# A decoder block with 9984 large float32r products: their operands laid at other distances modulo 512 bytes

## The chip, the cores and the metric

One core of one Trainium2 chip runs the whole program. The metric is the device time of one execution in microseconds, the median of three runs.

## What is computed

The input x is 32 sequences of 64 tokens, 512 wide (2048 tokens). Three layers are added to it in turn, each on a layer norm of what stands before it:

```python
x = x + attn(layernorm(x))    # a state space layer (Mamba-2 form), 128 heads of 64, 8 groups
x = x + xattn(layernorm(x))   # attention over 64 context tokens, 32 heads, 8 key/value heads
x = x + ffn(layernorm(x))     # four low-rank experts of rank 16, the two best by a router
```

The first layer is nearly all of the work:

```python
proj = input_states @ in_proj_w.T                  # 512 -> 8192 gate, 10240 xBC, 128 dt
xBC = silu(conv(xBC, 4 taps) + conv_b)             # 8192 x, 8 x 128 B, 8 x 128 C
dt = softplus(dt + dt_bias)
y = ssd(x, -exp(A_log), B, C, D, dt)               # causal over the 64 tokens, in chunks of 32
g = y * silu(gate)
g = g * rsqrt(mean of g*g in each of 8 groups + eps) * norm_w
return g @ out_w.T                                 # 8192 -> 512
```

## The kernel before, in words

The 2048 tokens are cut into four blocks of 512 (`tb`), and each block goes through the eight groups of the state space layer (`g`): 32 iterations `n`, in the order of the two Python loops of `iterations`. An iteration has 18 units of 128 projected channels: B, C, and eight pairs of x and gate. Each engine has one queue written out by hand, with semaphores between them, in the function `body` of its block; nothing is scheduled by a planner.

On TensorE an iteration holds, interleaved with each other:

- `unit(k, ...)`, line 538: a unit is a sum of 12 products of the helper `mm` (L472), 128x128 stationary by 128x512 moving, into one PSUM bank. Weights and normalised tokens are each split into a high and a low float32r part, and three of the four pairs are multiplied (`for w, a in ((0, 0), (0, 1), (1, 0))`) over four slices of the 512 inner channels. The stationary operand is a slice of `w_ring`, the moving one a slice of `xnb0` in even blocks and of `xnb1` in odd ones. 32 x 18 x 12 = 6912 products. In the first iteration four units go to the banks `p_out`, 48 products; the others go to `p_in`.
- `project(c, ...)`, line 789 (and 881 at the end): the output product. The stationary operand is a 128-token slice of the gated rows, `g_hi` (twice) and `g_lo` (once); the moving one is 512 columns of the output weights in `o_ring`. 12 products for each of eight `c`, 32 x 8 x 12 = 3072.
- `heads`, `state_products`, `to_tokens` (transposes of `x_t` against `id_sb`, L562), `mean_squares` (`ss` against `ones`) and, in `slot`, the pieces of the second and third layer (tiles `..._l`).
- `step_sizes(b)`, line 490, once a block: 12 products of the same form, `wd` stationary and `xnb` moving.

In block 0 the weights come raw from memory: SyncE loads `raw_w` (five slots, so five units ahead), ACT casts the high part into `w_ring` (six slots), POOL makes the low part (L1848), and SyncE stores both for the later blocks, which load `w_ring` directly. `o_ring` is filled in the same manner from `raw_o`.

A tensor is laid in each partition's memory in the order of its `sb(...)` call; `ExitStack`s give back ranges, so that the tiles of the second and third layer at the end (`tail`) overlay the loop's. `sb` aligns to 64 bytes (32 for tensors under 256 bytes) unless `align` is given:

```python
w_ring = sb("w_ring", [P, RING_W, 2, KT, P], F32R, align=2048)
xnb = [sb(f"xnb{b}", [P, 2, KT, TB], F32R, align=2048) for b in range(2)]
o_ring = sb("o_ring", [P, RING_O, 2, HID], F32R, align=2048)
g_hi = sb("g_hi", [P, 2, TB], F32R, align=2048)
g_lo = sb("g_lo", [P, 2, TB], F32R, align=2048)
```

Every slice of these tensors that a product reads is a multiple of 512 bytes from the tensor's start (128 or 512 elements of 4 bytes), so its place modulo 512 is the tensor's. "Distance" in this text is the moving operand's start less the stationary one's, modulo 512:

| product | stationary, mod 512 | moving, mod 512 | distance |
|---|---|---|---|
| units, all blocks | w_ring 0 | xnb 0 | 0 |
| output | g_hi, g_lo 0 | o_ring 0 | 0 |
| step sizes | wd 320 | xnb 0 | 192 |

Of the kernel before, what the change touches and what calls it, by code (L numbers as in the profile page):

```python
# [7 lines left out]
P = 128  # L8
NSEQ, SEQ, HID = 32, 64, 512
TOKENS = NSEQ * SEQ  # L10
KT = HID // P
# [3 lines left out]
CPG = INTER // GROUPS // P  # L15
TB = 512
NTB = TOKENS // TB
SPB = TB // SEQ
QT = TB // P
# [4 lines left out]
KV, REP, HD = 8, 4, 16  # L24
EXPERTS, RANK = 4, 16
LORA_SCALE = 16.0 / 16.0 ** 0.5
MIDW = EXPERTS * RANK
# [6 lines left out]
RING_W, RING_O = 6, 4  # L34
# [4 lines left out]
def decoder_kernel(nc, x, ctxv, amask, wt, wdt, owt, params, dtb, alog, ffa, ffb,  # L39
                   ident, c_mask, c_bd, c_v2, c_eq, out):  # L40
    F32, F32R = mybir.dt.float32, mybir.dt.float32r
# [8 lines left out]
    with outer:  # L50
        def alloc(stack):
            def sb(name, shape, dt=F32, align=None):
                wide = 4 * int(np.prod(shape[1:])) >= 256
                return stack.enter_context(nc.sbuf_tensor(name, shape, dt, align_bytes=align or (64 if wide else 32)))
            return sb

        def sem(name):
            return outer.enter_context(nc.semaphore(name))

        sb = alloc(outer)  # L60
# [7 lines left out]
        wa = sb("wa", [P, KT, MIDW + EXPERTS])  # L68
        cmask = sb("cmask", [P, SEQ])
        cpar = sb("cpar", [P, 5 * CONVS])  # L70
        dpar = sb("dpar", [P, CPG])
        dts = sb("dts", [P, QT, HPG])
        msv = sb("msv", [P, QT])
        rms = sb("rms", [P, QT])
        st6 = sb("st6", [P, QT, 6])
        mv = sb("mv", [P, QT, 2])
        ve = sb("ve", [P, QT])
        rstd = sb("rstd", [P, QT])
        spare = sb("spare", [P, 1])
        dtbs = sb("dtbs", [P, 1])  # L80
        als = sb("als", [P, 1])
        nega = sb("nega", [P, 3])
        acb = sb("acb", [P, 2, QT, HID], align=2048)
        wb = sb("wb", [MIDW, HID])

# [7 lines left out]
        sb = alloc(main)  # L93
# [2 lines left out]

        loop = ExitStack()
        sb = alloc(loop)
        xnb = [sb(f"xnb{b}", [P, 2, KT, TB], F32R, align=2048) for b in range(2)]
        dtk = sb("dtk", [P, 2, QT, HEADS])  # L100
        cumk = sb("cumk", [P, 2, QT, HEADS])
        decay = sb("decay", [P, 2, 8, QT, SEQ])
# [5 lines left out]
        sg = sb("sg", [P, GATES, TB])  # L108
        t_y = sb("t_y", [P, 2, TB])
        g_f = sb("g_f", [P, 2, TB])  # L110
        o_ring = sb("o_ring", [P, RING_O, 2, HID], F32R, align=2048)
        g_hi = sb("g_hi", [P, 2, TB], F32R, align=2048)
        g_lo = sb("g_lo", [P, 2, TB], F32R, align=2048)
        g_sq = sb("g_sq", [P, 2, TB])
        ss = sb("ss", [P, TB])
        cbt = sb("cbt", [P, QT, SEQ])
# [5 lines left out]
        d_s = sb("d_s", [P, TB])  # L122
        cum = sb("cum", [P, TB])

        VW = 2 * HD + 2
        TILE_WIDE = (("sc", [2, 2, 2 * KV // 2, SEQ]), ("row", [HID]), ("col", [KT, P]), ("x2s", [HID]))
        TILE_REST = (("p_t", [REP, KV // 2, P]), ("ctx", [P]), ("ctx_t", [P]), ("v2r", [2, P]), ("v2", [2, KV // 2, VW]), ("kbd", [2, KV // 2, SEQ]),
                     ("mid", [MIDW + EXPERTS]), ("midg", [MIDW]), ("m_t", [P]), ("mx", [REP * KV]), ("sm", [REP * KV]), ("rs", [REP * KV]),
                     ("st", [6]), ("mv", [2]), ("ve", [1]), ("rd", [1]), ("nm", [1]), ("nb", [1]), ("pw", [EXPERTS * EXPERTS]), ("pe", [EXPERTS * EXPERTS]),
                     ("rank", [EXPERTS]), ("lmax", [1]), ("gates", [EXPERTS]), ("gsum", [1]))  # L130
        Tile = namedtuple("Tile", [name for name, _ in TILE_WIDE + TILE_REST])

        def tile_part(sb, part, tag):
            return {name: sb(f"{name}_{tag}", [MIDW if name == "m_t" else P] + shape) for name, shape in part}

        rest = tile_part(sb, TILE_REST, "l")
        raw = ExitStack()
        sb = alloc(raw)
        raw_w = sb("raw_w", [P, RAW_W, KT * P])
        raw_o = sb("raw_o", [P, RAW_O, HID + 1])  # L140
        raw.close()
        wide = ExitStack()
        loop_tile = Tile(**tile_part(alloc(wide), TILE_WIDE, "l"), **rest)
        wide.close()
        loop.close()
# [2 lines left out]

        tail = ExitStack()
        sb = alloc(tail)  # L150
        tail_tiles = [Tile(**tile_part(sb, TILE_WIDE, q), **tile_part(sb, TILE_REST, q)) for q in range(QT)]
        tail.close()

        const_in = sem("const_in"); const_cp = sem("const_cp"); par_in = sem("par_in")
# [315 lines left out]
        def _(pe):  # L470
            def mm(o, l, r, first, last):
                return nc.tensor.matmul(o, lhsT=l, rhs=r, start=first, stop=last)  # L472
# [242 lines left out]
            def values_totals(q, t, S, banks):  # L715
# [4 lines left out]
                for r in range(REP):  # L720
                    for gp in range(KV // 2):
                        at = (r % 2 * (KV // 2) + gp) * VW
                        for s in range(2):
                            rows = slice(s * SEQ, (s + 1) * SEQ)
                            ins = mm(banks[r // 2][rows, at:at + VW], S.p_t[:, r, gp, rows], S.v2[:, s, gp, :], True, True)
                ins.then_inc(pv_done, 1)
# [213 lines left out]
        def _(act):  # L940
            def copy(dst, src, func=ACT.Copy, **kw):
                return nc.scalar.activation(dst, src, func, **kw)  # L942
# [296 lines left out]
            def ones_out(S):  # L1239
                by_pair = v2m[:, 0:2 * HD:HD].unsqueeze(1)  # L1240
                for s in range(2):
                    ins = copy(S.v2[:, s, :, 2 * HD:VW], by_pair.broadcast_to([P, KV // 2, 2]))
                ins.then_inc(v1_done, 1)
# [53 lines left out]
        def _(dve):  # L1297
# [4 lines left out]
            def link(ins):  # L1302

                own[0] += 1
                ins.then_inc(dve_own, 1)
                dve.wait_ge(dve_own, own[0])
# [313 lines left out]
            def attended_totals(t, S, banks):  # L1620

                dve.wait_ge(pv_done, t + 1)
                by_pair = [bank[:, 0:2 * (KV // 2) * VW].rearrange("p (r g c) -> p r g c", r=2, g=KV // 2) for bank in banks]
                for b in range(2):
                    ins = V.reciprocal(S.rs[:, b * 2 * KV:(b + 1) * 2 * KV].rearrange("p (r g e) -> p r g e", r=2, g=KV // 2),
                                       by_pair[b][:, :, :, 2 * HD:VW])
                link(ins)
# [445 lines left out]
```

## Time and profile before

| | |
|---|---|
| median of three runs | 2847.14 us (2843.8 to 2848.58) |
| the profiled execution's own time | 2843.42 us |
| its span, first to last instruction | 2841.6 us |
| granted TensorE clock over the span | 0.997 |
| TensorE matmuls | 22298, busy 2804.8 us |
| TensorE weight loads | 22298, busy 2274.4 us |
| VectorE (DVE) / ScalarE (ACT) / GpSimd (POOL) busy | 1990.1 / 1462.6 / 1315.5 us |
| mean transfer rate | 203 GB/s |

The profile is of one execution, taken by the hardware. A matmul's own time overlaps with that of the next one, so the sum of a group's busy time counts each stretch once, and the mean time of one matmul is longer than the step from its start to the next start. Weight loads stand as an engine of their own (PEld), since they run beside the matmul before them. In the chain of waits each piece of time is put to what ended last there.

### The profile page before, as it was taken

How to read it: one execution, taken by the hardware profiler on the slowest of the kernel's cores; microseconds unless marked ns; L12 is line 12 of the kernel's file. 1: busy time of each engine (PE TensorE's matmuls, PEld its weight loads, DVE VectorE, ACT ScalarE, POOL GpSimd, SP SyncE). 2: the span in 40 equal slices, each digit the busy share in tenths (PEclk: the TensorE clock that was granted, in tenths of full speed). 3: DMA queues.
4: the chain of work that ended last, by engine and by line, in shares of the span. 5: the costliest groups of instructions: out<-in, count | busy, mean ns of one | idle time of the engine just before them, and what ended most of it. 6: DMA issues, size and time to landing. Idle time of an engine off the chain costs nothing.

```text
span 2841.6 us, 56494 instructions
## 1 busy us (share of the span) xinstructions
PE 2804.8 (99%) x22298; PEld 2274.4 (80%) x22298; DVE 1990.1 (70%) x3152; ACT 1462.6 (51%) x2205; POOL 1315.5 (46%) x840
## 2 busy tenths in 40 slices
PE   7999999999999999999999999999999999999998
PEld 5788888878788788887888888888888888878886
DVE  8777768887667757677676766677666666666767
ACT  5666656655445545445445454544545444453545
POOL 4766767775344333443343443424434334343334
PEclk9999999999999999999999999999999999999999
DMA  7788777778565555565665665555656656555530
GB/s 253 274 298 300 264 270 258 269 257 291 181 200 189 181 183 182 181 192 182 203 193 180 200 189 174 186 180 185 203 180 192 193 173 203 181 184 187 186 130 31
DMA packets 179428, 578.27 MB, mean 203 GB/s; under 512 B 25248, under 2 KB 31904, under 8 KB 171104
## 3 DMA queue, kind: packets, MB, share of 16 engines
q1 hardware_dynamic: 179168, 574.66, 61.5%
q8 instruction: 180, 2.95, 0.4%
q14 instruction: 80, 0.66, 0.1%
HBM read 460.29 MB, written 114.29 MB: 202 GB/s over the span
## 4 chain that ended last, share of the span: by engine, by line
PE 91%; DVE 6%; ACT 1%; issue 1%; DMA 0%; POOL 0%; SPq 0%; DVEq 0%; ACTq 0%; POOLq 0%
PE p_in L472 53%; PE p_out L472 23%; PE p_y L472 9%; PE p_in L562 4%; DVE cv L1430 1%; PE p_y L700 1%; DVE o_ring L1370 1%; DVE t_y L1479 0%; DVE g_f L1491 0%; DVE mx L1600 0%; ACT cv L942 0%; DVE sc L1587 0%; DVE cum L1392 0%; DMA raw_w<-wt 0%; DVE decay L1462 0%
## 5 line engine op out<-in xcount | busy, mean ns | idle before, releaser
L472 PE MATMUL p_in<-xnb,w_ring 128*128 128x512 f32 x6864 | 1673.2, 396 | 1.8 <-DVE cv L1430 0.9
L472 PEld LDWEIGHTS p_in<-xnb,w_ring 128*128 128x128 f32 x6864 | 1260.8, 188 | 262.6 <-issue 2.7
L1430 DVE SCALAR_TENSOR_TENSOR cv<-p_in,cpar,cv 128x504 f32<-128x504 f32 x954 | 699.8, 734 | 469.2 <-ACT cv L942 445.4
L1856 POOL TENSOR_TENSOR g_lo<-g_f,g_hi 128x512 fp32r<-128x512 f32 x256 | 338.1, 1322 | 1195.8 <-ACT g_hi L942 1195.8
L472 PE MATMUL p_out<-o_ring,g_hi 128*128 128x512 f32 x2048 | 638.3, 393 | 1.7 <-POOL g_lo L1856 1.7
L942 ACT ACTIVATE cv<-p_in,cpar 128x512 f32<-128x512 f32 x318 | 246.6, 775 | 636.9 <-PE p_in L472 600.5
L472 PEld LDWEIGHTS p_out<-o_ring,g_hi 128*128 128x128 f32 x2048 | 379.4, 188 | 80.3 <-issue 2.3
L472 PE MATMUL p_out<-o_ring,g_lo 128*128 128x512 f32 x1024 | 399.6, 390 | 0.0
L1467 DVE TENSOR_TENSOR x_tok<-p_in,dts 128x512 f32<-128x512 f32 x256 | 176.5, 689 | 285.7 <-PE p_in L562 284.0
L942 ACT ACTIVATE x_t<-cv 128x512 f32<-128x512 f32 x256 | 160.9, 628 | 309.9 <-DVE t_y L1479 285.9
L1867 POOL TENSOR_TENSOR ss<-ss,g_sq 128x512 f32<-128x512 f32 x190 | 310.3, 1633 | 7.4
L1911 POOL TENSOR_TENSOR decay<-decay,cumk 128x2048 f32<-128x2048 f32 x63 | 234.8, 3727 | 38.9 <-DMA decay<-cum_scr 37.7
L942 ACT ACT_TABLE_LOAD x183 | 234.8, 1283 | 4.0 <-PEq L2067 0.7
L1848 POOL TENSOR_TENSOR w_ring<-raw_w,w_ring 128x512 fp32r<-128x512 f32 x144 | 209.2, 1477 | 51.5 <-ACT w_ring L942 35.8
L942 ACT ACTIVATE sg<-p_in 128x512 f32<-128x512 f32 x254 | 149.3, 588 | 160.9 <-PE p_in L472 160.9
L472 PEld LDWEIGHTS p_out<-o_ring,g_lo 128*128 128x128 f32 x1024 | 192.2, 188 | 40.7
L1479 DVE SCALAR_TENSOR_TENSOR t_y<-x_t,dpar,p_y 128x256 f32<-128x256 f32 x512 | 210.9, 474 | 1.1 <-PE p_y L472 1.1
L1491 DVE TENSOR_TENSOR g_f<-t_y,sg 128x512 f32<-128x512 f32 x256 | 180.2, 744 | 0.1
L942 ACT ACTIVATE g_hi<-g_f 128x512 fp32r<-128x512 f32 x256 | 159.2, 623 | 32.8 <-DVE g_f L1491 32.3
L472 PEld LDWEIGHTS p_y<-decay,x_tok 64*64 64x64 f32 x8192 | 131.1, 134 | 46.2 <-issue 46.2
L562 PE MATMUL p_in<-id_sb,x_t 128*128 128x128 f32 x1024 | 158.7, 278 | 7.1 <-ACT x_t L942 5.2
L562 PEld LDWEIGHTS p_in<-id_sb,x_t 128*128 128x128 f32 x1024 | 118.2, 141 | 51.5 <-issue 20.6
(258 smaller groups left out, 2251.4 us busy)
## 6 DMA issues: line engine op xcount, KB each, us to landing
w_ring<-ws_scr SPq DMA_DIRECT2D x432, 512.0 KB, 3.7
o_ring<-ows_scr SPq DMA_DIRECT2D x192, 512.0 KB, 4.6
ws_scr<-w_ring SPq DMA_DIRECT2D x144, 512.0 KB, 5.9
decay<-cum_scr SPq DMA_DIRECT2D x126, 512.0 KB, 6.7
raw_w<-wt SPq DMA_DIRECT2D x144, 256.0 KB, 5.1
ows_scr<-o_ring SPq DMA_DIRECT2D x64, 512.0 KB, 6.3
raw_o<-owt SPq DMA_DIRECT2D x64, 256.5 KB, 5.6
acb<-x SPq DMA_DIRECT2D x3, 1024.0 KB, 7.7
```

The costliest lines, as they stand in the source:

```text
L472: return nc.tensor.matmul(o, lhsT=l, rhs=r, start=first, stop=last)
L562: ins = nc.tensor.transpose(p_in[1][:, q * P:(q + 1) * P], x_t[:, c % 2, q * P:(q + 1) * P], id_sb[:, :])
L700: ins = nc.tensor.transpose(banks[rl][:, gp * P:(gp + 1) * P], pv, id_sb[:, :])
L942: return nc.scalar.activation(dst, src, func, **kw)
L1430: ins = V.scalar_tensor_tensor(acc[:, :, t:SEQ], src[:, :, 0:SEQ - t], cpar[:, 5 * m + 3 - t:5 * m + 4 - t], acc[:, :, t:SEQ], ALU.mult, A ...
L1467: V.tensor_tensor(x_tok[:, c % 2, :, :].rearrange("p q (h d) -> p q h d", h=2), p_in[1][:, :].rearrange("p (q h d) -> p q h d", q=QT, h=2) ...
L1479: ins = V.scalar_tensor_tensor(t_y[:, c % 2, :].rearrange(by_seq, q=QT, s=2)[:, s], x_t[:, c % 2, :].rearrange(by_seq, q=QT, s=2)[:, s], d ...
L1491: V.tensor_tensor(g_f[:, c % 2, :], t_y[:, c % 2, :], sg[:, (CPG * n + c) % GATES, :], ALU.mult).then_inc(g_done, 1)
L1848: T(w_ring[:, k % RING_W, 1, :, :].rearrange("p k c -> p (k c)"), raw_w[:, (UNITS * g + k) % RAW_W, :], w_ring[:, k % RING_W, 0, :, :].rea ...
L1856: T(g_lo[:, c % 2, :], g_f[:, c % 2, :], g_hi[:, c % 2, :].bitcast(F32), ALU.subtract).then_inc(glo_done, 1)
L1867: T(ss[:, :], a, g_sq[:, c % 2, :], ALU.add).then_inc(ss_done, 1)
L1911: T(decay[:, blk, :, :, :], decay[:, blk, :, :, :], last.unsqueeze(3).broadcast_to([P, 8, QT, SEQ]), ALU.subtract) \
```

## The change

The tensors are laid out anew; nothing else is touched. The small tensors `ve`, `rstd`, `spare`, `dtbs` (128 bytes together) come before `xnb0`, `st6` and `mv` (128 bytes) between `xnb0` and `xnb1`, and `dpar`, `msv`, `rms`, `als` (128 bytes) between `o_ring` and `g_hi`. The alignment to 2048 falls away for `xnb`, `o_ring`, `g_hi` and `g_lo`, and stays for `w_ring` and `acb`. Five small tiles of the second and third layer (`mx`, `sm`, `rs`, `pw`, `pe`) move ahead of `acb`, into the room that the others left.

```diff
-        xnb = [sb(f"xnb{b}", [P, 2, KT, TB], F32R, align=2048) for b in range(2)]
+        xnb = []
         ve = sb("ve", [P, QT])
         rstd = sb("rstd", [P, QT])
         spare = sb("spare", [P, 1])
         dtbs = sb("dtbs", [P, 1])
+        xnb.append(sb("xnb0", [P, 2, KT, TB], F32R))
+        st6 = sb("st6", [P, QT, 6])
+        mv = sb("mv", [P, QT, 2])
+        xnb.append(sb("xnb1", [P, 2, KT, TB], F32R))
...
-        o_ring = sb("o_ring", [P, RING_O, 2, HID], F32R, align=2048)
-        g_hi = sb("g_hi", [P, 2, TB], F32R, align=2048)
-        g_lo = sb("g_lo", [P, 2, TB], F32R, align=2048)
+        o_ring = sb("o_ring", [P, RING_O, 2, HID], F32R)
+        dpar = sb("dpar", [P, CPG])
+        msv = sb("msv", [P, QT])
+        rms = sb("rms", [P, QT])
+        als = sb("als", [P, 1])
+        g_hi = sb("g_hi", [P, 2, TB], F32R)
+        g_lo = sb("g_lo", [P, 2, TB], F32R)
...
+        loop_small = tile_part(sb, TILE_SMALL, "l")
         acb = sb("acb", [P, 2, QT, HID], align=2048)
         wb = sb("wb", [MIDW, HID])
...
-        rest = tile_part(sb, TILE_REST, "l")
+        rest = {**tile_part(sb, TILE_REST, "l"), **loop_small}
```

The places that come out of it:

| product | stationary, mod 512 | moving, mod 512 | distance |
|---|---|---|---|
| units, even blocks (0, 2) | w_ring 0 | xnb0 128 | 128 |
| units, odd blocks (1, 3) | w_ring 0 | xnb1 256 | 256 |
| output | g_hi, g_lo 384 | o_ring 256 | 384 |
| step sizes, even blocks | wd 192 | xnb0 128 | 448 |
| step sizes, odd blocks | wd 192 | xnb1 256 | 64 |

The tensors behind them move along: `dtk` to `g_f` from 0 to 256 modulo 512, `g_sq`, `ss` and `cbt` from 0 to 384, `raw_w` and `raw_o` from 256 to 128. All five engines issue the same instructions in the same order, with the same waits.

## Rows read from the trace of the kernel before

**Rows 1.** The page: busy us of each engine, share of the span, instructions.
```profile
PE 2804.8 (99%) x22298; PEld 2274.4 (80%) x22298; DVE 1990.1 (70%) x3152; ACT 1462.6 (51%) x2205; POOL 1315.5 (46%) x840
```
**Rows 2.** The page: the chain that ended last, by engine and by line.
```profile
PE 91%; DVE 6%; ACT 1%; issue 1%; DMA 0%; POOL 0%; SPq 0%; DVEq 0%; ACTq 0%; POOLq 0%
PE p_in L472 53%; PE p_out L472 23%; PE p_y L472 9%; PE p_in L562 4%; DVE cv L1430 1%; PE p_y L700 1%; DVE o_ring L1370 1%; DVE t_y L1479 0%; DVE g_f L1491 0%; DVE mx L1600 0%; ACT cv L942 0%; DVE sc L1587 0%; DVE cum L1392 0%; DMA raw_w<-wt 0%; DVE decay L1462 0%
```
**Rows 3.** Waits of TensorE, longest first: us in total, times, longest us.
```profile
PE p_out L478 <- DVE t_y L1338: 10.1, 1, 10.1
PE p_in L562 <- ACT x_t L942: 5.2, 7, 1.3
PE p_y L500 <- DVE d_s L1400: 2.9, 1, 2.9
```
**Rows 4.** Waits of all engines, longest first.
```profile
ACT cv L942 <- PE p_in L472: 600.5, 220, 6.0
...
DVE x_tok L1467 <- PE p_in L562: 284.0, 159, 4.0
```
**Rows 5.** Stretches: length, busy us of each engine, granted clock, DMA share, GB/s.
```profile
0.00:100.00 100.00, 77.60 (x528) 62.21 (x529) 80.91 (x115) 60.05 (x93) 54.83 (x39) 0.95 0.82 276
100.00:690.00 590.00, 586.60 (x4437) 477.30 (x4436) 450.51 (x623) 357.89 (x557) 414.65 (x255) 1.00 0.80 275
...
2100.00:2790.00 690.00, 688.80 (x5543) 559.72 (x5544) 450.39 (x742) 329.01 (x493) 270.09 (x178) 1.00 0.55 177
```
**Rows 6.** Groups by form: count | busy us, mean ns of one | idle before.
```profile
L472 PE MATMUL p_in<-xnb,w_ring 128*128 128x512 f32 x6864 | 1673.2, 396 | 1.8 <-DVE cv L1430 0.9 <-DVE x_tok L1467 0.9
L472 PEld LDWEIGHTS p_in<-xnb,w_ring 128*128 128x128 f32 x6864 | 1260.8, 188 | 262.6 <-issue 2.7
L472 PE MATMUL p_out<-o_ring,g_hi 128*128 128x512 f32 x2048 | 638.3, 393 | 1.7 <-POOL g_lo L1856 1.7
L472 PE MATMUL p_out<-o_ring,g_lo 128*128 128x512 f32 x1024 | 399.6, 390 | 0.0
...
L700 PE MATMUL p_y<-id_sb,sc_l 128*128 128x128 f32 x192 | 24.8, 272 | 0.0
...
L700 PEld LDWEIGHTS p_y<-id_sb,sc_l 128*128 128x128 f32 x192 | 22.4, 140 | 3.1
...
L472 PE MATMUL p_y<-xnb,wd 128*128 128x512 f32 x48 | 11.9, 397 | 0.8 <-ACT xnb L942 0.8
L472 PE MATMUL p_out<-xnb,w_ring 128*128 128x512 f32 x48 | 11.0, 389 | 0.0
```
**Rows 7.** TensorE, 1055.60 to 1058.05 us: the group, then its timeline row.
```profile
L472 PE MATMUL p_in<-xnb,w_ring 128*128 128x512 f32 x13 | 3.1, 389 | 0.0
...
1055.24 3.11 PE L472 MATMUL p_in<-xnb,w_ring 128*128 128x512 f32 x13
```
**Rows 8.** Timeline of TensorE, 999 to 1003 us, output products and transposes.
```profile
999.90 0.39 PE L472 MATMUL p_out<-o_ring,g_lo 128*128 128x512 f32 x1
1000.13 0.62 PE L472 MATMUL p_out<-o_ring,g_hi 128*128 128x512 f32 x2
...
1001.94 0.39 PE L472 MATMUL p_out<-o_ring,g_lo 128*128 128x512 f32 x1
1002.17 1.03 PE L700 MATMUL p_y<-id_sb,sc_l 128*128 128x128 f32 x8
```
**Rows 9.** Timeline of TensorE about two runs of step sizes.
```profile
1077.97 0.39 PE L472 MATMUL p_out<-o_ring,g_lo 128*128 128x512 f32 x1
1078.19 2.96 PE L472 MATMUL p_y<-xnb,wd 128*128 128x512 f32 x12
1080.99 1.00 PE L472 MATMUL p_y<-wa,col_l 128*128 128x68 f32 x8
...
1774.89 2.96 PE L472 MATMUL p_y<-xnb,wd 128*128 128x512 f32 x12
1777.69 1.00 PE L472 MATMUL p_y<-wa,col_l 128*128 128x68 f32 x8
```
**Rows 10.** Timeline of TensorE, 1052 to 1062 us, a run of 24 unit products.
```profile
1052.62 5.74 PE L472 MATMUL p_in<-xnb,w_ring 128*128 128x512 f32 x24
1058.19 0.95 PE L472 MATMUL p_y<-ones,ss 128*128 128x1 f32 x8
1059.00 0.72 PE L472 MATMUL p_out<-o_ring,g_hi 128*128 128x512 f32 x2
...
1060.48 0.60 PE L732 MATMUL p_y<-id_sb,row_l 128*128 128x128 f32 x4
```
**Rows 11.** The same timeline cut at 1053.0 us, the run's first two.
```profile
1052.62 0.71 PE L472 MATMUL p_in<-xnb,w_ring 128*128 128x512 f32 x2
```
**Rows 12.** The page: the cast that reads raw_w, and the issues of its loads.
```profile
L942 ACT ACTIVATE w_ring<-raw_w 128x512 fp32r<-128x512 f32 x144 | 81.4, 618 | 0.5 <-DMA raw_w<-wt 0.5
...
raw_w<-wt SPq DMA_DIRECT2D x144, 256.0 KB, 5.1
```

More of the change, by code:

```diff
@@ L70, in decoder_kernel, with tile_part @@
         cpar = sb("cpar", [P, 5 * CONVS])
-        dpar = sb("dpar", [P, CPG])
         dts = sb("dts", [P, QT, HPG])
[L73 to L81, printed above, removed]
-        nega = sb("nega", [P, 3])
+        nega = sb("nega", [P, 3])
+        VW = 2 * HD + 2
+        TILE_WIDE = (("sc", [2, 2, 2 * KV // 2, SEQ]), ("row", [HID]), ("col", [KT, P]), ("x2s", [HID]))
+        TILE_REST = (("p_t", [REP, KV // 2, P]), ("ctx", [P]), ("ctx_t", [P]), ("v2r", [2, P]), ("v2", [2, KV // 2, VW]), ("kbd", [2, KV // 2, SEQ]),
+                     ("mid", [MIDW + EXPERTS]), ("midg", [MIDW]), ("m_t", [P]),
+                     ("st", [6]), ("mv", [2]), ("ve", [1]), ("rd", [1]), ("nm", [1]), ("nb", [1]),
+                     ("rank", [EXPERTS]), ("lmax", [1]), ("gates", [EXPERTS]), ("gsum", [1]))
+        TILE_SMALL = (("mx", [REP * KV]), ("sm", [REP * KV]), ("rs", [REP * KV]), ("pw", [EXPERTS * EXPERTS]), ("pe", [EXPERTS * EXPERTS]))
+        Tile = namedtuple("Tile", [name for name, _ in TILE_WIDE + TILE_REST + TILE_SMALL])
+        def tile_part(sb, part, tag):
+            return {name: sb(f"{name}_{tag}", [MIDW if name == "m_t" else P] + shape) for name, shape in part}
+        loop_small = tile_part(sb, TILE_SMALL, "l")
         acb = sb("acb", [P, 2, QT, HID], align=2048)
@@ L98, in decoder_kernel @@
         sb = alloc(loop)
-        xnb = [sb(f"xnb{b}", [P, 2, KT, TB], F32R, align=2048) for b in range(2)]
+        xnb = []
+        ve = sb("ve", [P, QT])
+        rstd = sb("rstd", [P, QT])
+        spare = sb("spare", [P, 1])
+        dtbs = sb("dtbs", [P, 1])
+        xnb.append(sb("xnb0", [P, 2, KT, TB], F32R))
+        st6 = sb("st6", [P, QT, 6])
+        mv = sb("mv", [P, QT, 2])
+        xnb.append(sb("xnb1", [P, 2, KT, TB], F32R))
         dtk = sb("dtk", [P, 2, QT, HEADS])
@@ L123, in decoder_kernel @@
         cum = sb("cum", [P, TB])
[L125 to L134, printed above, removed]
-        rest = tile_part(sb, TILE_REST, "l")
+        rest = {**tile_part(sb, TILE_REST, "l"), **loop_small}
         raw = ExitStack()
@@ L150, in decoder_kernel @@
         sb = alloc(tail)
-        tail_tiles = [Tile(**tile_part(sb, TILE_WIDE, q), **tile_part(sb, TILE_REST, q)) for q in range(QT)]
+        tail_tiles = [Tile(**tile_part(sb, TILE_WIDE, q), **tile_part(sb, TILE_REST + TILE_SMALL, q)) for q in range(QT)]
         tail.close()
```

## The prediction

> **What bounds the kernel now.** I read the page's busy times first, then the chain that ended last, the costliest groups, and the timeline of TensorE at a few places. TensorE's matmuls cover 99% of the span and no other engine covers more than 70% [rows 1]. The chain lies on TensorE for 91%, 53% in the projections of the units and 23% in the output products, both from the helper at L472 [rows 2]. TensorE waits 10.1 us once for the very first normalised rows, 5.2 us in seven waits for x_t, and under 3 us for anything else [rows 3], while ACT and DVE wait for it by hundreds of us [rows 4]. Its clock is granted at 1.00 from 100 us to 2790 us, the 2.4 GHz level, and at 0.95 in the first 100 us [rows 5]. So the kernel's time is the number of matmuls by the time from one start to the next. Nothing else is near: a shorter pace shortens the kernel one to one, and so does a longer one.
>
> The large products are 6864 + 48 of the units and 2048 + 1024 of the output [rows 6], 9984 in all, each with a weight load of its own of 188 ns that runs beside the matmul before it. The "busy" ns of such a matmul (396) is no pace, since neighbours overlap. The pace is read from starts. In the middle of a run of unit products, 13 matmuls cover 3.11 us; less the last one's 0.389 that is 12 steps of **226.8 ns** [rows 7]. Output products: from 999.90 to 1002.17 there are ten starts, 227.0 ns each [rows 8]. All these have moving and stationary operand at distance 0 modulo 512.
>
> The trace also holds one product of the same form at another distance: the step sizes, where wd begins at 320 and xnb at 0, so 192 apart. Twelve of them start at 1078.19 and the next work at 1080.99: 2.80 / 12 = **233.3 ns**; at 1774.89 to 1777.69 it is again 2.80 us [rows 9]. Both times the run is entered straight from output products at 227 ns, under the same clock, with nothing waited for. The same 128x512 product is 6.5 ns (3%) slower there. No other row shows a product of this form at a distance other than 0, and the forecast leans on it.
>
> One more thing is in the rows. A run of 24 unit products that follows transposes starts at 1052.62, and the next work starts at 1058.19: 5.57 us, or 232.1 ns each [rows 10]. Its first two cover 0.71 us, so the first step is 0.71 - 0.39 = 0.32 us, an exposed load [rows 11]. The other 23 take 5.25 us, 228.3 ns each, though the second half of the run goes at 226.8: the pace starts slower and settles. At distance 0 there is a rhythm into which loads and matmuls fall; 192 did not fall into it in 12 products.
>
> **The change part by part.** No instruction is added, removed or moved on any engine; only addresses differ. The pieces:
>
> Unit products: distance 128 in even blocks, 256 in odd ones. No row shows either. From below, I bound the pace by the shortest step in the rows, 0.22 us, from the last output product at 1077.97 to the first step-size product at 1078.19 [rows 9]. From above I take twice the step from 226.8 to 233.3, so 240 ns. The value I take is 233.3, from the only row at a non-zero distance. A run of 24 then takes 0.32 + 23 x 0.2333 = 5.69 us against 5.57, so 0.11 to 0.12 more; 6912 / 24 = 288 such runs give **+32 us**, 16 in even and 16 in odd blocks.
>
> Output products: stationary g_hi and g_lo at 384, moving o_ring at 256, so 384 apart. By the same row each goes from 226.8 to 233.3. Of the 96 of a group, 78 follow other large products and are already in the rhythm; the 12 and the 6 that follow short ones begin slower (from 1059.00 to 1060.48 six take 1.48 us [rows 10]) and lose perhaps 1 ns. 32 x (78 x 6.5 + 18 x 1) ns = **+17 us**. None of this has cover: ACT and DVE wait for TensorE, not the reverse [rows 3, 4].
>
> Step sizes: distances 448 and 64 for 192. There are 48 products [rows 6]; even 7 ns each is 0.3 us. Nothing.
>
> Short matmuls, transposes and heads change their distances too. Their steps are set by other things: eight transposes cover 1.03 us, so (1.03 - 0.27) / 7 = 109 ns for 128 columns with a load of 140 ns each [rows 6, 8]: nothing is seen lost there, though their operands are 384 apart, so I put nothing, and 2 us in either direction.
>
> Loads of raw_w: its address goes from a multiple of 256 to 128 past one. There are 144 of them with 5.1 us to landing, and the cast that reads them waited 0.5 us in all for them, because they are issued five units ahead [rows 12]. Were each load an eighth longer, that would be 0.6 us within that slack: nothing.
>
> Sum: 2843.4 (the profiled execution's own time) + 32 + 17 = **2892 us**. That execution lies 3.7 us below the median of the three runs, 0.13%, so I leave the figure as it is.
>
> The Trainium skill has a rule that speaks against any effect: its page "SBUF — State Buffer", section "Who interferes with whom", says that TensorE has two independent read ports, one for the moving operand and one for weight loads, and that it never waits on anyone. Taken so, the distance cannot matter and the sum is 0. The rows at 192 speak against it, by 6.5 ns in 227, though they hold one product only.
>
> **The rivals.**
>
> *Slower, but in part.* One or two of the three distances keep the 226.8 and the others go to 233.3: +16 to +33 us, so 2859 to 2876. For it: three distances are unlikely to behave exactly alike.
>
> *Much slower.* A step twice as large, 240 ns: of the 9984 products some 9300 are not the first of a run (each of the 32 groups has about 20 runs in the program's order), and from 228.3 ns now they lose 11.7 ns each: +109 us, so 2952. Nothing in the rows shows a run at 240.
>
> *No change (the distance counts modulo 128 or less, or not at all).* 128, 256 and 384 are multiples of 128, while the only slow row, 192, is 64 past one. If what counts is the distance modulo 128, all three stay at 226.8 and the time stays at 2843 to 2847. The skill's two ports, read strictly, give the same. For it: the 109 ns of the transposes, whose operands are a multiple of 128 apart, show nothing lost; nothing excludes it. Against: the run's slow start shows that loads and matmuls do disturb each other even at distance 0.
>
> *Faster.* The mechanism: at distance 0 load and matmul begin on the same 512-byte phase and may hold each other up at once; with the operands apart that meeting goes away. The place is every product inside a run. If only the slow beginnings of runs vanish, a run of 24 takes 0.32 + 23 x 0.2268 = 5.54 us, 0.03 to 0.04 less: -11 us and 2832. If the pace goes to 220 ns, the bound from below, it is 9300 x 8.3 ns = -77 us and 2766. It decides from a settled pace under 226. For it: the slow beginnings show that something is lost when load and matmul meet badly, so a better meeting may exist. The Trainium skill's page "TensorE: Matmul & The Clock Gate", section "Wait — 56ns, not 53.3ns?", gives 215.7 ns for back-to-back 512-column matmuls at the full clock, so by that page some 11 ns per product could be won; its estimate would be near -117 us. Against: the rows show no run under 226.8, and the one other distance went the wrong way. Most likely here is one group of the three gaining: 2820 to 2832.
>
> **How the numbers follow.** About 0.2% (6 us) is what a measurement of this kernel can tell from no change. Forecast (all three at about 233): 0.42. Slower in part: 0.12. Much slower: 0.04. No change: 0.18. Faster: 0.24. So slower 0.58, same 0.18, faster 0.24. The range runs from 2805, which takes in a gain in one or two groups but not the full one (0.08 left below), to 2925, which takes in a pace of some 236.5 ns (0.06 left above). The likeliest case alone would be 2880 to 2905.
>
> **What would show it.** Right: unit products in the settled part of a run at 233 ns in place of 226.8, output products at 233 in place of 227.0, the group's busy sum up by about 32 + 17 us, and waits of DVE and ACT for TensorE longer. Even blocks (0 to 690 us, 1400 to 2100 us) against odd ones tell 128 from 256; the output products tell 384; the step sizes tell 448 and 64. Right for the rhythm as a cause: 24 products that no longer settle. Wrong: a pace still at 226.8 in all three (the modulus is 128 or less), or a run of 24 in under 5.5 us (the distance helps). A longer first quarter with an unchanged pace would mean that the loads of raw_w, not the products, changed.

## The result

The changed kernel takes 2868.64 us (median of four runs, 2866.74 to 2873.24) against 2845.47 us for the kernel before, run beside it. The ratio is 1.0084, with a 95% interval from 1.0066 to 1.0102: slower by about 24 us. It is the rival "slower, but in part", forecast at 2859 to 2876 with a chance of 0.12; the figure forecast as likeliest was 2892.

### The profile page after: what moved, and what is told of

The parts are those of the page before. It is cut to its first block, busy times and chain, and to the rows that moved or that the text cites. A ratio compares the mean times of both kernels' runs of the same rounds, so it can differ in the third digit from the quotient of the medians.

```text
span 2867.4 us, 56494 instructions
## 1 busy us (share of the span) xinstructions
PE 2833.6 (99%) x22298; PEld 2280.3 (80%) x22298; DVE 1988.4 (69%) x3152; ACT 1465.4 (51%) x2205; POOL 1315.7 (46%) x840
## 4 chain that ended last, share of the span: by engine, by line
PE 92%; DVE 5%; ACT 1%; issue 1%; DMA 0%; POOL 0%; SPq 0%; DVEq 0%; ACTq 0%; POOLq 0%
PE p_in L476 53%; PE p_out L476 24%; PE p_y L476 9%; PE p_in L566 4%; DVE cv L1434 1%; PE p_y L704 1%; DVE o_ring L1374 0%; DVE t_y L1483 0%; DVE g_f L1495 0%; DVE mx L1604 0%; DVE sc L1591 0%; DMA raw_w<-wt 0%; ACT cv L946 0%; PE p_y L736 0%; PE p_y L643 0%
## 5 line engine op out<-in xcount | busy, mean ns | idle before, releaser
L476 PE MATMUL p_out<-o_ring,g_hi 128*128 128x512 f32 x2048 | 649.2, 398 | 1.6 <-POOL g_lo L1860 1.6
L946 ACT ACTIVATE cv<-p_in,cpar 128x512 f32<-128x512 f32 x318 | 246.4, 775 | 653.7 <-PE p_in L476 614.9
```

## The profile after

The page's busy times and the groups by form, as in [rows 1] and [rows 6] (the lines of the kernel lie four further down):

```profile
PE 2833.6 (99%) x22298; PEld 2280.3 (80%) x22298; DVE 1988.4 (69%) x3152; ACT 1465.4 (51%) x2205; POOL 1315.7 (46%) x840
```

```profile
L476 PE MATMUL p_in<-xnb,w_ring 128*128 128x512 f32 x6864 | 1688.3, 398 | 1.8 <-DVE cv L1434 0.9 <-DVE x_tok L1471 0.9
L476 PE MATMUL p_out<-o_ring,g_hi 128*128 128x512 f32 x2048 | 649.2, 398 | 1.6 <-POOL g_lo L1860 1.6
L476 PE MATMUL p_out<-o_ring,g_lo 128*128 128x512 f32 x1024 | 404.3, 395 | 0.0
```

The same number of instructions; TensorE is busy 28.8 us longer, 15.1 of them in the unit products and 15.6 in the output products (a run's busy time reaches to the end of its last matmul, so the groups overlap a little). The other engines work as long as before and wait longer for TensorE, ACT 614.9 us for 600.5 [rows 4].

Stretches tell the distances apart. The next fence is the view of stretches for the instructions that touch w_ring alone, first of the kernel before, blocks 1, 2 and 3, then of the changed one. Columns: from:to, length, then busy us (count) of TensorE, of its loads, of ACT and POOL, then clock, DMA share and GB/s. The stretches are cut so that each holds the 1728 unit products of its block.

```profile
688.00:1383.00 695.00, 420.63 (x1728) 317.21 (x1728) 0.00 (x0) 0.00 (x0) 1.00 0.58 187
1383.00:2080.00 697.00, 420.59 (x1728) 317.21 (x1728) 0.00 (x0) 0.00 (x0) 1.00 0.59 188
2080.00:2780.00 700.00, 420.56 (x1728) 317.22 (x1728) 0.00 (x0) 0.00 (x0) 1.00 0.56 180
```

```profile
696.00:1395.00 699.00, 421.60 (x1728) 317.21 (x1728) 0.00 (x0) 0.00 (x0) 1.00 0.58 185
1395.00:2102.00 707.00, 427.44 (x1728) 317.92 (x1728) 0.00 (x0) 0.00 (x0) 1.00 0.57 185
2102.00:2800.00 698.00, 421.59 (x1728) 317.21 (x1728) 0.00 (x0) 0.00 (x0) 1.00 0.56 180
```

An even block (distance 128) pays 6.8 us, an odd one (256) 1.0 us. The loads' own busy time stays, 317 us. The same view for o_ring, before and after, in block 2, with DVE between the loads and ACT:

```profile
1383.00:2080.00 697.00, 188.10 (x769) 142.96 (x768) 0.00 (x0) 0.00 (x0) 1.00 0.59 188
```

```profile
1395.00:2102.00 707.00, 191.77 (x769) 143.22 (x768) 0.00 (x0) 0.00 (x0) 1.00 0.57 185
```

Output products (384) pay 3.7 us per block. The timeline of TensorE shows it in runs that answer to [rows 10]. Four pieces of the changed kernel: units in block 0 (distance 128) and in block 1 (256), a run of step sizes at 64 and one at 448. (`step_sizes(tb + 1)` is called in the block before its own, so the run at 401.93 us, in block 0, reads `xnb1` and the one at 1088.28 us, in block 1, reads `xnb0`.)

```profile
376.47 5.83 PE L476 MATMUL p_in<-xnb,w_ring 128*128 128x512 f32 x24
382.13 0.95 PE L476 MATMUL p_y<-ones,ss 128*128 128x1 f32 x8
...
1062.67 5.74 PE L476 MATMUL p_in<-xnb,w_ring 128*128 128x512 f32 x24
1068.25 0.95 PE L476 MATMUL p_y<-ones,ss 128*128 128x1 f32 x8
...
401.93 2.91 PE L476 MATMUL p_y<-xnb,wd 128*128 128x512 f32 x12
404.68 0.49 PE L566 MATMUL p_in<-id_sb,x_t 128*128 128x128 f32 x3
...
1088.28 2.96 PE L476 MATMUL p_y<-xnb,wd 128*128 128x512 f32 x12
1091.08 1.01 PE L476 MATMUL p_y<-wa,col_l 128*128 128x68 f32 x8
```

From the start of 24 unit products to the next work it is 5.66 us at 128 and 5.58 us at 256, against 5.57 at 0. Step sizes go at 2.75 / 12 = 229 ns at 64 and at 2.80 / 12 = 233.3 at 448.

Start to start in ns, read from the trace inside such runs, the pace is a rhythm that repeats:

```
distance 0 (before, units and output):  227 226 227 227 226 227 ...            mean 226.7
distance 256 (after, odd blocks):       227 226 227 227 226 227 ...            mean 226.7
distance 128 (after, even blocks):      241 233 231 231 229 230 232, repeated  mean 232.4
distance 384 (after, output):           241 233 231 231 229 230 232, repeated  mean 232.4
```

Not every run at 128 goes so: of the 78 runs of 24 unit products in the changed kernel's even blocks, 16 alternate 238 and 229 (mean 233.3) in place of it.

One part of the difference between the two profiled executions is none of the change. The first step sizes, before and after:

```profile
14.47 3.04 PE L472 MATMUL p_y<-xnb,wd 128*128 128x512 f32 x12 [0.78 <-ACT xnb L942]
```

```profile
14.30 5.01 PE L476 MATMUL p_y<-xnb,wd 128*128 128x512 f32 x12 [0.78 <-ACT xnb L946]
```

In the second most of them went at 427 ns each, the 1.2 GHz level. The trace records the clock's first rise at 18.65 us there and at 13.52 us in the execution of before; TensorE had done only its first sixteen transposes when it rose before, and in the changed kernel's execution it was at the tenth of the step sizes. (Ahead of the first record the view of stretches prints 1.00, which is no measurement.) The traces of e1 and e10, where units and output products are at distance 0, show the same 427 ns and a first rise at 18.5 us, so it is not the distance that makes it. It makes 2 of the 25.8 us between the spans.

## The experiments

**Place or distance?** In the changed kernel the slow operands are also the ones that start at 128 modulo 256 (xnb0, g_hi, g_lo); xnb1, at 256, is nearly free. So the place of a single operand would explain everything too. In e1 everything large starts at 128:

```diff
-        w_ring = sb("w_ring", [P, RING_W, 2, KT, P], F32R, align=2048)
+        ve = sb("ve", [P, QT])
+        rstd = sb("rstd", [P, QT])
+        spare = sb("spare", [P, 1])
+        dtbs = sb("dtbs", [P, 1])
+        w_ring = sb("w_ring", [P, RING_W, 2, KT, P], F32R)
```

with `st6` and `mv` put behind `g_lo`, and `o_ring`, `g_hi`, `g_lo` one behind the other.

> Weights, tokens, output weights and gated rows all start at 128 modulo 512, so the distance is 0 again for units and output (step sizes 448). Theory D (the distance between the operands counts): units and output products settle at 226.7 ns per step as before, time within 0.2% of before, 2843 to 2848 us. Rival P (the place of an operand counts, 128 past a multiple of 256 is slow): units of all four blocks and output at about 232.4 ns, +12 for even blocks, +12 for odd, +14 for output, about 2883 us. Rival N (the neighbours that moved along count, not these operands): something in between, with no settled 226.7.

Measured: 2844.95 us against 2843.7, ratio 1.0002 (0.9992 to 1.0012). The view of stretches for w_ring and then o_ring, block 2 of e1:

```profile
1385.60:2082.40 696.80, 420.67 (x1728) 317.18 (x1728) 0.00 (x0) 0.00 (x0) 1.00 0.58 187
...
1385.60:2082.40 696.80, 187.90 (x768) 142.97 (x768) 0.00 (x0) 0.00 (x0) 1.00 0.58 187
```

Unit products to 0.1 us those of the kernel before (whose 188.10 us for `o_ring` holds one product more). The place falls. So do the neighbours, which had moved here as well: `g_sq`, `ss`, `cbt`, `raw_w` and `raw_o` stand where they do in the changed kernel, and `dtk` to `g_f` at 128 (in e6 below they stand at the changed kernel's 256). What is left is the distance.

**The parts alone.** e2 leaves xnb0 and xnb1 at 0 and has output weights at 0, gated rows at 128 (the 128 bytes of `dpar` to `als` between them). e3 has xnb0 alone at 128, with 256 bytes more ahead of xnb1, and all else at 0:

```diff
         xnb.append(sb("xnb0", [P, 2, KT, TB], F32R))
         st6 = sb("st6", [P, QT, 6])
         mv = sb("mv", [P, QT, 2])
+        pad0 = sb("pad0", [P, 64])
         xnb.append(sb("xnb1", [P, 2, KT, TB], F32R))
```

> Output products alone at distance 384 (g at 128, output weights at 0), units at distance 0. D: output steps at about 232.4 ns, units settle at 226.7; +14 us, 2857 to 2861. P (place of the stationary operand): the same here. If output products stay at 226.7 the pair 384/256 of the changed kernel was slow for its places.

> Units of even blocks alone at distance 128 (tokens at 128), odd blocks and output at 0. D and P alike: units of blocks 0 and 2 at about 232.4 ns, the rest settles at 226.7; +12 us, 2855 to 2859. With the output part (e2) and the odd blocks' +2 us it should add up to the 23 us of the whole change; if it does not, the parts are not independent.

Measured: e2 1.0068 (1.0051 to 1.0086), +19 us; e3 1.0044 (1.0029 to 1.0059), +12.5 us. e2's block 2, w_ring then o_ring:

```profile
1391.80:2093.10 701.30, 421.67 (x1728) 317.24 (x1728) 0.00 (x0) 0.00 (x0) 1.00 0.58 186
...
1391.80:2093.10 701.30, 191.93 (x768) 143.50 (x768) 0.00 (x0) 0.00 (x0) 1.00 0.58 186
```

and e3's, where block 1 is undisturbed at 420.55 and 187.89:

```profile
1387.40:2092.00 704.60, 427.10 (x1728) 317.91 (x1728) 0.00 (x0) 0.00 (x0) 1.00 0.58 185
...
1387.40:2092.00 704.60, 189.79 (x768) 142.97 (x768) 0.00 (x0) 0.00 (x0) 1.00 0.58 185
```

The output's 4.0 us per block (against e1's 187.90) and the units' 6.5 us are there, but each part also costs its neighbour: in e2 the units, at distance 0, pay 1.1 us a block, and in e3 the output products, at distance 0, pay 1.9 us in the even block. So e2 lies above the 2857 to 2861 that I expected; e3, at 2855.2, is in its range. Since the two kinds follow each other without a break, a run is entered out of the other's rhythm and needs some products to find its own. The starts show it: of the runs of 24 unit products that follow output products directly, all 16 in blocks 1 and 2 of the kernel before step at 226 and 227 ns from the first on, and all 24 in blocks 1 to 3 of e2 take seven other steps first (236, 224, 231, 235, 229, 232, 231 ns in the one at 1401.61 us).

The parts add up to 32 us and the whole is 24. By the traced executions, blocks 0 to 2 of e2 and e3 together are 24.8 us longer than before, and those of the changed kernel 20.2 (block 2: 4.6 + 7.9 against 10.0). That the cost of entering is not paid on both sides where both kinds are off would fit, but no run tests it alone. The rest of the gap lies in the last block and the tail, where the clock stood at the 1.2 GHz level for 15.3 us in e2's trace and 11.0 in e3's, and for 5.4 in the changed kernel's.

**256 for all.** e6: xnb0, xnb1 and o_ring at 256, w_ring and the gated rows at 0 (a `pad0` of 128 bytes beside `dpar` to `als`).

> Units of all blocks and output products at distance 256. If the distance counts modulo 256, everything settles at 226.7 ns and the time is that of before, 2841 to 2850 us (ratio 0.998 to 1.002). If 256 costs something of its own (the odd blocks of the changed kernel stood at 228.9 against 228.4), units go to 228.9 and the time rises by 3 to 5 us; the rival is that those 0.5 ns came from the output products at 384 between the units, as in e2, and then they are gone here.

Measured: 1.0004 (0.9994 to 1.0014). Block 2, w_ring then o_ring:

```profile
1382.90:2079.60 696.70, 420.62 (x1728) 317.17 (x1728) 0.00 (x0) 0.00 (x0) 1.00 0.58 188
...
1382.90:2079.60 696.70, 187.92 (x768) 142.94 (x768) 0.00 (x0) 0.00 (x0) 1.00 0.58 188
```

256 is free, and the 1.0 us that the odd blocks of the changed kernel paid came from the output products between the units.

**A map.** e4, e5, e7 and e8 put other padding before xnb0, xnb1 and between output weights and gated rows; the two finer ones ask for an alignment of 32 or 16 bytes. One execution each. e4's edit:

```diff
+        pad0 = sb("pad0", [P, 16])
+        xnb.append(sb("xnb0", [P, 2, KT, TB], F32R))
+        st6 = sb("st6", [P, QT, 6])
+        mv = sb("mv", [P, QT, 2])
         xnb.append(sb("xnb1", [P, 2, KT, TB], F32R))
```

and 64 bytes more ahead of the gated rows. e5: xnb0 at 320, xnb1 at 448, the gated rows ahead of the output weights at 448 and 0. e7: xnb0 at 32, xnb1 at 96, output 128 and 160. e8: xnb0 at 16, xnb1 at 48, output 64 and 64.

> Map: units even 64, odd 192, output 320. If only the distance modulo 256 counts, even blocks give the 233.3 ns of the step sizes at 64, odd blocks and the 192 of before also 233.3, and output at 320 is as 64, 233.3: about +45 us, 2890. If each distance is its own case, the three differ; none is expected under 226.7.

> Map: units even 320, odd 448, output 64. The step sizes at 448 showed 229.0 ns and at 64 233.3. So odd blocks at 229, output at 233.3, even blocks open: 233.3 if 320 is as 64, 229 if it is as 448. About +35 to +45 us, 2880 to 2890. Chance 0.15 that one of them settles under 226.7.

> Finer map: units even 32, odd 96, output 480 (224 modulo 256). If the pace is a smooth function of the distance modulo 256, even blocks lie between 226.7 and 229, odd ones between 229 and 233, output between 233 and 226.7. If only whole 64-byte steps count, 32 is as 0 or 64. Chance 0.2 that one settles under 226.7.

> Finer map: units even 16, odd 48, output 0 (both at 64). Output settles at 226.7 since its distance is 0. Even and odd blocks between 226 and 230; an even pace of 226.7 at 16 would mean that the rhythm has some width.

Measured: 2866.44 us (e4) and 2866.26 (e5) against 2840.55; 2887.95 (e7) and 2867.73 (e8) against 2842.46. The view of stretches for w_ring, blocks 1 and 2, of e4, e5, e7 and e8:

```profile
690.00:1394.20 704.20, 428.62 (x1728) 316.99 (x1728) 0.00 (x0) 0.00 (x0) 1.00 0.57 184
1394.20:2094.00 699.80, 422.21 (x1728) 317.28 (x1728) 0.00 (x0) 0.00 (x0) 1.00 0.58 187
```

```profile
689.00:1394.10 705.10, 428.81 (x1728) 316.98 (x1728) 0.00 (x0) 0.00 (x0) 1.00 0.57 184
1394.10:2094.50 700.40, 422.67 (x1728) 317.26 (x1728) 0.00 (x0) 0.00 (x0) 1.00 0.58 187
```

```profile
695.20:1401.70 706.50, 428.82 (x1728) 317.25 (x1728) 0.00 (x0) 0.00 (x0) 1.00 0.57 184
1401.70:2109.50 707.80, 428.16 (x1728) 316.84 (x1728) 0.00 (x0) 0.00 (x0) 1.00 0.58 185
```

```profile
692.50:1394.50 702.00, 426.06 (x1728) 317.55 (x1728) 0.00 (x0) 0.00 (x0) 1.00 0.58 185
1394.50:2097.80 703.30, 426.16 (x1728) 317.63 (x1728) 0.00 (x0) 0.00 (x0) 1.00 0.58 186
```

Put together, for the 1728 unit products of a block, against 420.6 us at 0:

| distance | run | busy us per block | more | settled rhythm, mean ns |
|---|---|---|---|---|
| 0 | before, e1 | 420.6 | | 226.7 |
| 16 / 48 | e8 | 426.2 / 426.1 | 5.6 / 5.5 | 230 to 233 |
| 32 / 96 | e7 | 428.2 / 428.8 | 7.6 / 8.2 | 233 |
| 64 | e4 | 422.2 | 1.6 | 229.0 |
| 128 | e3, after | 427.1, 427.4 | 6.5, 6.8 | 232.4 |
| 192 | e4 | 428.6 | 8.0 | 233.3 |
| 256 | e6 | 420.6 | 0.0 | 226.7 |
| 320 | e5 | 422.7 | 2.1 | 229.0 |
| 448 | e5 | 428.8 | 8.2 | 233.3 |

Distances 256 apart behave alike (0 and 256, 64 and 320, 192 and 448, and with the output products 128 and 384). Within 256 the pace is no smooth function, as one half of my expectation for e7 had it: 64 is cheap, 32 and 96 beside it are not. The sign matters too: 64 is cheap and 192, its mirror, is not. I had expected 233.3 at 64 and got 229.0, so e4 and e5 came out some 20 us shorter than I put them. That was a misreading of the changed kernel's trace: both expectations have its two runs of step sizes exchanged, the 229 ns belonging to 64 and the 233.3 to 448, as shown above. The expectations for the finer map missed too: 32 settles at 233.3 and not between 226.7 and 229, and 16 settles at 231.7 and 48 at 230.0 or 233.3, where I had set 230 as the bound. The output products of e8, at distance 0, come back to 226 and 227 ns as expected where a run is long enough. None settles under 226.7.

The distance does not fix the rhythm alone. At 64 and 320 most runs go at 229.0, but in block 1, beside units at 233.3, 11 of the 48 runs of 12 output products that directly follow units in e4 (320), and 16 of 48 in e5 (64), end at 233.3; and e2's step sizes, at 320 as well, go at 233.3 in three of their four runs. Which of two rhythms a run falls into seems to hang on how it is entered. At 0 and 256 every run of 24 in blocks 1 to 3 came back to 226.7.

**Is it the weight load?** e9 is the changed kernel with half loads in 7 of 12 unit products, which then also compute half of the channels:

```diff
+                        m = P if j < KT or j == 3 * KT - 1 else SEQ
-                        ins = mm(in_bank(k, n), w_ring[:, k % RING_W, w, kt, :], ...
+                        ins = mm(in_bank(k, n)[0:m, :], w_ring[:, k % RING_W, w, kt, 0:m], ...
```

> The changed kernel, but 7 of the 12 products of a unit load and compute 64 of the 128 channels only, so half of the projected channels are a partial sum; the moving operand is as before. If the extra time over the columns is the clash of a product's reads with the next weight load, it falls with half a load: steps inside those 7 under 226 ns, nearer 220, and the difference between even (128) and odd (256) blocks shrinks. If the extra is a matter of the moving reads or the array alone, the steps stay at 232 and 226.7.

Measured: 2873.29 us, one execution. The view of stretches for w_ring, blocks 1 and 2, and the loads by form:

```profile
695.90:1395.60 699.70, 422.00 (x1719) 261.60 (x1717) 0.00 (x0) 0.00 (x0) 1.00 0.58 185
1395.60:2098.90 703.30, 424.12 (x1728) 263.72 (x1728) 0.00 (x0) 0.00 (x0) 1.00 0.58 186
```

```profile
L476 PEld LDWEIGHTS p_in<-xnb,w_ring 128*64 128x64 f32 x4004 | 538.6, 135 | 353.2 <-issue 0.8
```

The loads became 135 ns in place of 188, and the products did not get faster on the whole: per product 245.5 ns of busy time at distance 256 (422.00 / 1719; this stretch leaves out the first nine products of its block), where the full loads gave 244.0, and 245.4 at 128 (424.12 / 1728), where they gave 247.4. The steps inside the seven have means of 227 to 233 ns by their place in the unit, not near 220. So the first half of my expectation failed: the extra time is not in proportion to what is loaded. But the difference between 128 and 256 is gone, and the steps stayed neither at 232 nor at 226.7: in the second half of runs of 24 they average 230.8 at 128 and 230.6 at 256. So it is not a matter of the moving reads or the array alone either, unless the half-size product itself, which this edit does not separate from its load, changes the rhythm. That fits a meeting of two streams at a certain phase and not a loss per byte; what exactly meets is not shown.

**Does the identity matrix matter?** The kernel before, with `id_sb` and `v2m` exchanged, so that the moving operand of the transposes is at 0.

> The kernel before, with the identity matrix (moving operand of all transposes) at 0 modulo 512 in place of 128, v2m in its place. If the slow beginnings of runs come from entering the rhythm out of transposes at another distance, the units' mean step falls from 228.4 towards 226.7 and the time by up to 11 us, 0.4%. If they come from the exposed load at the start alone, nothing changes: ratio 0.999 to 1.001. I hold the second for likelier.

Measured: 0.9999 (0.9989 to 1.0008). Units 420.66 us in block 2, as before. The slow beginnings of runs stay; the transposes' distance is not their cause, as I had held likelier. No version beat the kernel before.

## Why the prediction was right in sign and half in size

*What bounds the kernel: right.* The time followed the pace of the large products. By the starts in the trace, block 1 lasts 699.3 us from its first unit product to the next block's, for 695.0 before, and block 2 706.6 for 696.7: +4.3 and +10.0 us. Block 0 grew by 6.0 only; TensorE stood idle there for 12.2 us where it had been 14.9, so some of its waiting was taken up. The last block with the tail grew by 3.8, with 5.4 us at the 1.2 GHz level where the execution before had 8.7. Together 24.0 us, and 1.8 for the clock at the start of this execution.

*Units at 128, +16 us for both even blocks: nearly right.* 2 x 6.8 = 13.6 us of busy time, at 232.4 ns in most runs for the 233.3 taken.

*Units at 256, +16 us: wrong, and the step that failed.* "The value I take is 233.3, from the only row at a non-zero distance" carried one distance over to all. 256 costs nothing of itself (e6), and 1.0 us a block for its neighbours, 2 us in both odd blocks for the 16 forecast. The slow run's beginning and the rhythm were read rightly, but one row at 192 could not say with which distance the rhythm comes back. The other two terms came out near their size, though they leaned on the same row: that 128 and 384 are about as slow as 192 is what the runs found, not what the row showed.

*Output at 384, +17 us: right,* 4 x 3.7 = 15 us of busy time. (The groups' 13.6 + 2 + 15 us are more than the span's 24.0, since neighbouring groups overlap and block 0 took up some waiting.)

*Step sizes, short matmuls, raw_w: nothing, right.* The raw loads land in 5.1 us as before, the transposes take 277 ns for 278.

*The bounds:* the settled pace stayed between 220 and 240 ns in the mean, though single steps of 241 ns occur.

*The rivals.* "No change" put the modulus at 128 or less. By the distances tried it is 256, so that rival was right for one of the three distances and wrong for two. "Faster" happened at no distance that was tried. The rule of the Trainium skill, page "SBUF — State Buffer", section "Who interferes with whom", is that TensorE's two read ports are independent and that it never waits on anyone. Taken as the prediction took it, that the distance cannot matter to the time, it does not hold here: with the same instructions and the same loads, 6912 + 3072 products took 24 us more by the distance of their operands alone, and with both moved together (e1) nothing. Whether it is the ports that meet, or something behind them, is not shown.

## What to carry to other kernels

Where a kernel is bound by 128x512 float32r products with a weight load each, lay the moving and the stationary operand at the same place modulo 256 bytes. An allocation that aligns to 64 bytes, as `sb` does here, leaves that to chance, and at the distances tried it cost up to 3% of the settled step (233.3 ns for 226.7) and 2% of the unit products' busy time (428.8 us for 420.6). Judge a layout by the step from start to start in the settled part of a run, and measure the very distance that is meant, since a row at another one says little of it. Products that follow each other without a break should share the rule: in e2 and e3 the kind left at distance 0 paid 1.1 and 1.9 us a block for entering from the other's rhythm.

## What the runs showed of the hardware

- The settled pace of 128x512 float32r products with their own loads depends on the distance of the operands modulo 256 bytes: 226.7 ns at 0 (before, e1, e6), 229.0 at 64 in most runs (e4, e5), 232.4 at 128 in most (after, e3), 233.3 at 192 (e4, e5).
- The pace is a repeating rhythm: 226 or 227 ns throughout at 0, a cycle of seven (mean 232.4) at 128, of three (226, 229, 232) at 64, of two (231, 236) at 192. One distance can have more than one: in even blocks of the changed kernel some runs at 128 went 238, 229, 238, 229, at 64 and 320 some went at 233.3, and at 192 both 231, 236 and a steady 233.3 occur.
- A shorter weight load (135 ns for 188) does not bring the step near 220 ns: 230.6 at 256 and 230.8 at 128, for 226.7 and 232.4 to 233.3 (e9).
- After transposes, the first step of a run of units is 311 to 324 ns, and at distance 0 up to eleven steps pass before the run is at 226 and 227 ns (before, blocks 1 and 2).
- Distances of 16 to 48 bytes, less than a 64-byte step, cost 5.5 to 7.6 us per block, more than 64 does (1.6).
